# A factorization-machine attention kernel: attention products of most steps in two half sums side by side

## The reference

```
inner = x[:, row] * x[:, col]                                        # 512 x 528 x 128, row < col of 33 fields
fm = relu(einsum('bpd,ad->bpa', inner, attn_W) + attn_b)             # 128 x 128 weights
scores = einsum('ba,bpa->bp', gnn_feature, fm)
attn = softmax(scores, axis=1)
attn_output = einsum('bp,bpd->bd', attn, inner) * 100.0
z = concatenate([gnn_feature, attn_output], axis=1)
h = concatenate([z, gnn_feature], axis=1)                            # 512 x 384
y = relu(relu(h @ W_top1 + b_top1) @ W_top2 + b_top2) @ W_top3
```

## Time and profile before

| | |
|---|---|
| median of three runs | 651.45 us |
| profiled execution | 656.16 us |
| its span | 654.4 us |
| TensorE busy | 641.9 us |
| ScalarE busy | 417.4 us |
| VectorE busy | 403.6 us |
| GpSimd busy | 268.8 us |

### The profile page before, as it was taken

One profiled execution on the slowest core, in us unless ns is written; L12 is line 12 of the kernel. 1 busy time (PEld: TensorE's weight loads), 2 busy tenths in 40 slices (PEclk: granted clock), 3 DMA queues, 4 the chain that ended last, 5 costly groups with the idle time before them and its releaser, 6 DMA issues.

```text
span 654.4 us, 22667 instructions
## 1 busy us (share of the span) xinstructions
PE 641.9 (98%) x9596; PEld 328.1 (50%) x9596; DVE 403.6 (62%) x426; ACT 417.4 (64%) x797; POOL 268.8 (41%) x208
## 2 busy tenths in 40 slices
PE   6998999999999999999999999999999999999998
PEld 2444444444444555544444555544444555544566
DVE  3564655656664677676655577766655567764763
ACT  2665666666777566676777556667677666677651
POOL 6787876685656422244746522244101011100010
PEclk9999999999999999999999999999999999999999
DMA  3211111011091111000092111000026011030010
GB/s 117 83 37 37 30 36 30 25 30 64 18 31 27 28 32 26 16 13 18 14 32 30 24 32 30 16 18 6 1 14 15 7 17 18 7 21 8 16 25 8
DMA packets 51286, 17.29 MB, mean 26 GB/s; under 512 B 47553, under 2 KB 48321, under 8 KB 51202
## 3 DMA queue, kind: packets, MB, share of 16 engines
q1 hardware_dynamic: 44738, 6.03, 11.3%
q0 software_dynamic: 4288, 8.66, 5.5%
q10 hardware_dynamic: 2176, 1.32, 0.7%
HBM read 14.10 MB, written 1.89 MB: 24 GB/s over the span
## 4 chain that ended last, share of the span: by engine, by line
PE 91%; DVE 2%; POOL 2%; DMA 2%; another core or an unknown queue 1%; issue 1%; ACT 0%; DVEq 0%; ACTq 0%
PE x_ps L466 66%; PE s_ps L478 16%; PE m_ps L531 4%; POOL rows L364 2%; DVE inner L757 2%; PE m_ps L523 1%; DMA rows<-in_table,idx 1%; PE s_ps L571 1%; PE x_ps L571 1%; PE x_ps L531 1%; DMA idx_in<-in_ids 0%; PE x_ps L560 0%; DVE e_t L809 0%; PE m_ps L560 0%
## 5 line engine op out<-in xcount | busy, mean ns | idle before, releaser
L700 ACT ACTIVATE fm<-x_ps,ab 128x352 f32<-128x352 f32 x768 | 406.0, 555 | 204.3 <-PE x_ps L466 184.2
L466 PE MATMUL x_ps<-inner,attn_w_t 128*32 128x352 f32 x6144 | 480.8, 459 | 2.2 <-issue 0.9
L466 PEld LDWEIGHTS x_ps<-inner,attn_w_t 128*32 128x32 f32 x6144 | 201.5, 110 | 229.7 <-issue 149.4
L757 DVE TENSOR_TENSOR inner<-e_t 128x2112 f32<-128x2112 f32 (+1 forms) x128 | 302.0, 2359 | 19.3 <-PE x_ps L466 16.6
L364 POOL DMA_INDIRECT rows<-in_table,idx x128 | 213.0, 1664 | 196.5 <-PE s_ps L478 179.9
L478 PE MATMUL s_ps<-fm,gnn_col 128*32 128x256 f32 (+1 forms) x2048 | 138.0, 386 | 0.0
L773 DVE COPY gnn_col<-gnn_z 128x8 f32<-128x8 f32 (+1 forms) x120 | 23.9, 199 | 180.0 <-PE s_ps L478 173.0
L478 PEld LDWEIGHTS s_ps<-fm,gnn_col 128*32 128x32 f32 x2048 | 68.7, 110 | 62.4 <-issue 20.5
L392 POOL TENSOR_TENSOR band<-band 128x192 f32<-128x192 f32 (+1 forms) x39 | 26.3, 676 | 145.6 <-DMA band<-band_scratch 145.1
L531 PE MATMUL m_ps<-band,rows 128*32 128x132 f32 x912 | 33.5, 275 | 0.0
L531 PEld LDWEIGHTS m_ps<-band,rows 128*32 128x32 f32 x912 | 27.9, 109 | 7.1
(11 more groups left out here) (57 smaller groups left out, 86.5 us busy)
## 6 DMA issues: line engine op xcount, KB each, us to landing
band<-band_scratch SPq DMA_DIRECT2D x144, 18.4 KB
rows<-in_table,idx POOLq DMA_INDIRECT x128, 2.5
band_scratch<-zeros SPq DMA_DIRECT2D x1, 784.0 KB, 3.3
w<-in_W_top ACTq DMA_DIRECT2D x3, 256.0 KB
band_scratch<-attn SPq DMA_DIRECT2D x12, 64.0 KB
gnn_z<-in_gnn_pairs SPq DMA_DIRECT2D x1, 512.0 KB
w<-in_W_top ACTq DMA_DIRECT2D x1, 512.0 KB
gnn_t<-in_gnn_cols SPq DMA_DIRECT2D x1, 256.0 KB, 3.8
```

Of the source, the lines that this page charges most:

```text
L466: mm = pe.matmul(strip(x_ps[:, (ROUNDS * slot + r) % 4, 0:ROUND], c), strip_of(attn_w_t, c), round_of(inner, slot, r), start=True, stop=True)
L700: act.activation(round_of(fm, slot, r), x_ps[:, (ROUNDS * slot + r) % 4, 0:ROUND], ACT.Relu, bias=ab[:, 0:1]).then_inc(fm_ready, 1)
L757: dve.tensor_tensor(inner[:, slot, :, :].rearrange("p q (i k) -> p q i k", k=HOPS), flat(e, at, [[P * WIDE, P], [WIDE, QUADS], [1, FIELDS] ...
```

## The change

The score of a pair is a sum over 128 outputs of the attention layer, weighted with the row's gnn feature g. In 79 of the 128 steps ("halved") this sum is now prepared by ScalarE and VectorE. A round of pair products puts outputs 64h to 64h + 63 for the first half of the pairs (hops 1 to 8) on partitions 0 to 63, and the same outputs for the other half of the pairs on partitions 64 to 127. ScalarE computes relu(|g| x + |g| b), with |g| and |g| b as scale and bias of each partition, into `rel`. VectorE adds the two output halves of a row, the second times the product of the two signs (`add_halves`: one scalar_tensor_tensor of 264 columns a row). The score matmul then has 264 columns a row, with the signs in two columns of a stationary `diag`, one for each half of the pairs. The other 49 steps ("full", `FULL`) keep the old sum, as two parts of 264 columns, with a sliding `window` for the stationary.

Score rows are now in pairs of partitions, 16 steps fill a region, and each of the two regions of a tile has a bank and a softmax stage of its own; `row_max` and `normalise` combine two neighbouring partitions by a shuffle. Attention is stored after each region. The last tile's second region is cut at step 28 (`LATE_M`). The products come as two instructions of 1056 columns. Wrapping in tile 0 moves from VectorE to GpSimd's queue (`FIRST_WRAPS`), which also computes signs, sizes and biases of the later tiles in nine operations (`weigh_later`). Sixteen identity matmuls (`WARM_UPS`) run ahead of the gnn layer, which moves to other banks. The last stores are shared among the queues of SyncE, ScalarE and GpSimd, the last loads between SyncE and GpSimd. The tail's pooling adds the wrapped columns by matmuls of their own (`pool_tail`) instead of GpSimd's fold. The MLP parts come in another order, and some buffers share memory.

```diff
+def is_full(n):
+
+    t, s = divmod(n, STEPS)
+    if n < OPENING_FULL or n == STEPS * TILES - 1:
+        return True
+    if t > 0 and POOL_AT <= s < TRANS_AT:
+        return s % 2 == 1
+    return s % 3 == 2
...
             for s in range(STEPS):
...
                 else:
+                    if s == AHEAD_AT:
+                        pool.wait_ge(bands_zeroed, 16)
                     gather_group(2, s - AHEAD_AT)
+                if s in FIRST_WRAPS:
+                    wrap(0, FIRST_WRAPS[s])
                 wraps(1, s)
...
+                weigh_later(s - WEIGH_AT)
...
+            def pair_products(n):
+
+                slot = n % 2
+                pe.wait_ge(inner_ready, SIDES * n + SIDES)
+                for q in range(QUADS):
+                    for h in range(SIDES):
+                        bank = 2 * (q % 2) + h
+
+                        if n == 0 and q == 1:
+                            pe.wait_ge(gnn_layer_read, C1)
+                        elif n > 0 or q >= 2:
+                            pe.wait_ge(rel_ready, ROUNDS * n + (2 * q + h - 3))
+                        for c in range(STRIPS):
+                            weights = strip_of(attn_w_t, c if FULL[n] else 2 * h + c % 2)
+                            mm = pe.matmul(strip(x_ps[:, bank, 0:HALF], c), weights,
+                                           inner[:, slot, h if FULL[n] else c // 2, q, :], start=True, stop=True)
+                        mm.then_inc(x_ready, 1)
...
+                else:
+                    pe.wait_ge(fm_ready, QUADS * halved_through(n))
+                    pe.wait_ge(diag_ready, n // 4 + 1)
                     for q in range(QUADS):
...
+                        mm = pe.matmul(s_ps[32 * q:32 * q + 32, r, 0:HALF], diag[:, m % REGION, q, :], fm[:, n % 2, q, :],
+                                       start=m % REGION == 0, stop=n + 1 in STAGE_END, skip_group_check=late)
...
+            for _ in range(WARM_UPS):
+                pe.matmul(x_ps[:, 0, 0:P], ident[:, :], ident[:, :], start=True, stop=True)
...
+            pe.wait_ge(tail_band_loaded[0], 16 * GROUP)
+            for k in range(EARLY_SETS):
+                pool_tail(k)
+            mlp_layer2(T2)
+            mlp_layer3(T2)
+            mlp_layer2(T01)
+            mlp_layer3(T01)
+            mlp_layer1(T3A)
...
+                        else:
+                            act.activation(rel[:, n % 2, q, h, :], x_ps[:, 2 * (q % 2) + h, 0:HALF], ACT.Relu,
+                                           bias=shift[:, h, b:b + 1], scale=size[:, h, b:b + 1]).then_inc(rel_ready, 1)
...
+            def add_halves(n):
+
+                t, m = divmod(n, STEPS)
+                if n >= 2:
                     dve.wait_ge(scores_done, n - 1)
...
+                for q in range(QUADS):
+                    b = P * t + QUADS * m + q
+                    dve.wait_ge(rel_ready, ROUNDS * n + 2 * q + 2)
+                    dve.scalar_tensor_tensor(fm[:, n % 2, q, :], rel[:, n % 2, q, 1, :], turn_sign[:, b:b + 1],
+                                             rel[:, n % 2, q, 0, :], ALU.mult, ALU.add).then_inc(fm_ready, 1)
...
+            for n in range(2, STEPS * TILES):
+                t, s = divmod(n, STEPS)
+                if n == CHUNK:
+                    dve.wait_ge(turn_copied, turns_through(0, 1))
+                if t == 0 and s > CHUNK and s % (2 * CHUNK) == 0:
+                    dve.wait_ge(wrapped, s // CHUNK)
+                if t > 0 and s == 0:
+                    dve.wait_ge(wrapped, CHUNKS * t + CHUNKS - 2)
+                product(n)
+                if n - 1 in STAGE_END and STAGE_END[n - 1] == OPEN_STAGE:
+                    row_max(OPEN_STAGE)
...
+                if FULL[n]:
+                    set_window(n)
+                if not FULL[n - 1]:
+                    add_halves(n - 1)
+                if n - 1 in STAGE_END and STAGE_END[n - 1] == OPEN_STAGE:
+                    normalise(OPEN_STAGE)
...
+                if n - 1 in STAGE_END and STAGE_END[n - 1] != OPEN_STAGE:
+                    row_max(STAGE_END[n - 1])
+                if n - 2 in STAGE_END and STAGE_END[n - 2] != OPEN_STAGE:
+                    normalise(STAGE_END[n - 2])
```

804 lines of the change are left out of this document (446 added, 358 removed).

## The result

The changed kernel takes 640.64 us (median of 4 runs, 639.56 to 641.54) beside 651.49 us for the kernel before (651.18 to 651.76). The ratio is 0.9836, 95% interval 0.9825 to 0.9848. So it is faster by 10.9 us, under 2%; the prediction said 23.4. Its profiled execution took 640.47 us (span 638.7 us), at its median, while that of the kernel before, 656.16 us, stood 4.7 us above its own. In the profile 15.7 us are gone, in the median 10.9, and this difference turns out to be part of the answer.

What follows compares the result with a forecast made beforehand. TensorE's streaming was taken as the bound, 4.44 us a step. Terms -33.9 - 1.5 + 1 + 2.4 + 3.0 - 0.5 + 6.1 = -23.4 us, from the median 651.45 to 628.0 us; 8 in 10 within 617 to 645.

Steps and rivals of the forecast that it cites:

- the stage ends: Softmax work on VectorE where regions end: TensorE waits add 2.4 us, and 3.0 us at the last tile's step-28 stage.
- the opening behind step 8: After step 8, GpSimd runs late by four steps with copy waits and nine weighing operations: +1 us (0 to +9).
- the shift from the profile to the median: The profiled execution stands 4.7 us above the median of the runs; the same difference turns 632.8 into 628.0 us.
- The signs that the prediction named for being wrong: On VectorE and GpSimd: adds starting more than 0.65 us apart, or gathers taking over 3 us each.
- Another of its signs: In the changed kernel's profile, TensorE still holds over 90% of the chain of waits, with VectorE near 85%.
- The halved scores: Scores of 79 steps in half the columns: 0.445 us saved each, 35.2 us; steps of 4.005 and 4.45 us.
- The pair products' added 1.3 us: Pair products in 8 rounds of 264 columns instead of 6 of 352: +0.01 us in each of 128 steps.
- The add: VectorE's add of 264 columns in halved steps occupies 0.34 us, four a step, covered by TensorE's time.
- The opening up to step 8: Gathers start 1.9 us earlier; at the end of step 8, -1.5 us beyond the steps' own saving (-4 to +2).
- The tail: After the last scores: pooling groups +3.7 us and waits between MLP layers +2.4, together +6.1 us (+2 to +9).
- GpSimd starved by half products: GpSimd gets in only when VectorE pauses, so gathers make product 8 and tile 1's turning late: 645 us, 15%.
- VectorE as the bound: VectorE bounds every halved step if an add takes 0.65 us or more; at 0.75 us, 660 us; 10%.

Runs made afterwards that it cites:

- The spacing alone: Changed kernel with GpSimd clearing a 512-column scratch row behind each gather of the first two tiles, from chunk 1 on: 657.37 us (kernel before 651.34).
- the four edits: Changed kernel with chunk 3's wrap behind chunk 2's, weighing on VectorE, four more whole steps at stage ends, reordered tail: 664.13, 663.77, 664.09 us (unaltered 670.07).
- the run on one queue: Changed kernel with all late stores and loads of the bands on SyncE's queue instead of three queues: 639.73 us (kernel before 651.34).

## Why the prediction was wrong, step by step

The forecast was 628.0 us and the result 640.6, so the gain was 10.9 us where 23.4 was forecast, and the miss is 12.6 us. Three steps failed: the stage ends, the opening behind step 8, and the shift from the profile to the median. The signs that the prediction named for being wrong didn't appear: adds stand 0.40 us apart and not 0.65, and of the 128 gathers two took over 3 us. Another of its signs did fail: TensorE was to hold over 90% of the chain, and holds 68%. By its own steps:

- **The halved scores, right.** 79 times 0.445 us: the steps are 4.00 and 4.45 us apart, as worked out. The pair products' added 1.3 us came too (a whole step is 4.45 us instead of 4.44). ScalarE was not in the way (581 and 482 ns beside rounds of 445, with overlap; it waited for TensorE).
- **The add, mis-sized.** It was taken at 0.34 us; four together take 1.70 to 1.78 us, 0.40 from start to start. In steady steps this is covered: VectorE's triple, forecast at 10.1 us, is some 10.4 (an estimate, from the 13.55 of the run with doubled adds less eight adds of 0.40), still under 12.46. It is not covered where a stage ends.
- **Stage ends, mis-sized: 2.4 and 3.0 us forecast, 9 measured.** Each tile start costs 1.2 us (0.9 forecast), three times. Step 19 costs 0.7, 0.9 and 0.3 us (0.3 forecast at step 20). Steps 4, 10, 26 and 29 of the tiles 1 and 2 cost 1.6 us that no term held. The open stage in tile 3 costs 2.0 us, against 3.0 forecast, and 1.0 of it also stands in the kernel with whole steps. What is left of the 10.4 us lost in these tiles, 1.4, is the moved pool groups and 0.01 us in each step. Halving's net worth is so 0.29 us a step at most, and not 0.43.
- **The opening up to step 8, nearly right, in part by luck.** Step 8 was to start at 53 to 57.5 us, behind the wrap copy that follows gather 26; it starts at 53.78. At the end of step 8 the traces have 0.9 us beyond the steps' own saving (step 9 starts at 60.66 us, for 63.21), and the text had 1.5. That the clock would fall, 2.9 us in step 8, stood nowhere. Without it 3.8 us would have been gained there, still within the text's -4 to +2.
- **The opening behind step 8, wrong in its mechanism: +1 us forecast, 3.0 measured.** The text let GpSimd run late by four steps, and TensorE wait for the last turned chunks. In the record no matmul of these steps waits for a gather. TensorE waits for VectorE's products: 1.7 us in step 17, where the row maximum comes in, 1.8 in step 20 and 0.6 ahead of step 27, as in the old kernel. (The 0.8 us by which step 12 and others are longer are turning matmuls, which the old kernel has too.) Their two half products stretch beside GpSimd's work, which the text had only for the gathers. At step 20, VectorE's two half products and GpSimd beside them:

```profile
111.73 4.13 DVE L902 TENSOR_TENSOR inner<-e_t 128x1056 f32<-128x1056 f32 x2
...
111.74 1.83 POOL L524 TENSOR_TENSOR size<-size,gnn_h 128x768 f32<-128x768 f32 x1
113.72 1.82 POOL L466 DMA_INDIRECT rows<-in_table,idx  x1 [0.16 <-issue]
```

The weighing operations were taken at 1 us each; they took 0.8 to 3.0:

```profile
L508 POOL TENSOR_SCALAR size<-gnn_h 128x768 f32<-128x768 f32 x1 | 3.0, 2977 | 0.0
...
L533 POOL TENSOR_SCALAR shift<-size,ab 128x384 f32<-128x384 f32 x2 | 2.6, 1322 | 0.1
```

VectorE's small operations beside them stretched too, as at 95 us: 0.98 us for a window copy that takes 0.16 elsewhere. The spacing alone also ended the stall of step 20, with the weighing still on GpSimd, so that the weighing by itself makes it is not shown.

```profile
92.47 2.63 DVE L902 TENSOR_TENSOR inner<-e_t 128x1056 f32<-128x1056 f32 x2
95.03 0.98 DVE L945 COPY window<-gnn_t 128x4 f32<-128x4 f32 x1
```

- **The shift from profile to median, wrong in kind.** The forecast took the record's 4.7 us over the median as a constant. The record agrees with one from a chip where the old kernel takes 655.3, and holds 29 of the bursts of increments that no record of the first kind has, so part of it is time that the timed runs never had, and that the change couldn't save. 4.9 us of the miss are this. They probably lie in the opening, as these bursts stand between 28.9 and 145.3 us; no trace of the old kernel on the first kind of chip was taken. The table of gains above compares a record of each kind in the same way.
- **The tail, right in its sum** (+6.1 us forecast, +6.2 measured from the first matmul behind the last scores, 28.8 us for 22.6), in part by luck: a group takes 0.35 us for 0.45, so the groups add 2.0 us for 3.7, and the waits went from 0.6 us to 3.8, where 1.3 and 3.7 had been taken. The 1.0 us left over is not traced. That three queues bring nothing was right as well.
- **The rivals.** GpSimd starved by half products (645 us) gave the time best and was still not the cause: the gathers became shorter, 1664 to 1165 ns, and what TensorE waited for was GpSimd's order at step 8 and VectorE's products after it. VectorE as the bound (660 us) came nearer than its 10% said: 0.65 us an add was the threshold, and with two adds of 0.40 it was the bound all through. A rival in which the chip turns the gain into a loss stood nowhere, and it is what happened in four of the five batches of experiments.

In sum, of the 12.6 us: 4.9 the shift, some 4.5 the stage ends and the steps beside them, some 2.6 the opening as recorded (0.6 up to step 8, 2.0 behind it). The rest is rounding and the tail.

The Trainium skill ("VectorE: DVE Perf Modes", section "The DRAIN you can't avoid") says that the next operation waits until the pipe is empty, and that one which is not held starts earlier. The prediction took only the first half and noted that the trace disagrees. The exception is what the adds show here: each is 0.49 us long, and four take 1.70, so they stand 0.40 us from start to start.

```profile
173.86 1.70 DVE L916 SCALAR_TENSOR_TENSOR fm<-rel,turn_sign 128x264 f32<-128x264 f32 x4
```

## What to carry to other kernels

When an engine goes from 62% to 87%, cost the change where it does its occasional work (stage ends, weighing, copies), not in the steady step: there the whole of the gain arrived, and in the other places 14.6 of its 34.7 us went. Read what stands in a row on GpSimd's queue ahead of whatever releases the others. Gaps between gathers in a row made 21.5 us on one kind of chip, with the four edits in, and cost 17 us on the other without them: try them on both. And before a profile's time is shifted to a median, ask if both come from the same kind of chip: a wait that the record shows and the timed runs don't have can't be won.

## What the runs showed of the hardware

- Two kinds of chip, as it seems, under one program: 651.4 or 655.3 us for the old kernel, and 640.6 or 670.1 for the new, so that even the sign of a change depends on the chip.
- On the second kind, increments of TensorE's semaphore are held while GpSimd issues gathers 1.26 us apart, come at steps of about 0.7 us, and then 0.09 us apart. With GpSimd clearing 512 columns (0.55 us) between them, the program with the four edits takes 21.5 us less (663.8 to 642.2).
- Behind 3.4 us without a matmul on TensorE the granted clock was at 1.2 GHz for 6.8 us, and 64 pair products took 6.2 us for 3.36. In the run on one queue a wait with 3.0 us idle brought 3.4 us at 1.2 GHz and 4.9 us for the products.
- A wrap copy of 256 columns, 0.41 us at the shortest, took 4.87 us on GpSimd beside four half products in a row, and ended behind them. Gathers that started during a product took 1.49 us in the mean with half products, 2.74 with whole ones.
- An activation with a scale for each partition takes 581 ns for 264 columns, one with a bias alone 482.
